# Closing quantised product of a fused transformer stack: the addition to X moved from GpSimd to VectorE, the exponents' scaling moved to ScalarE, exponent bits taken ahead

## What is computed

```
def quant_fp8(x):
    amax = jnp.max(jnp.abs(x)).astype(jnp.float32)
    scale = jnp.minimum(FP8_MAX / jnp.maximum(amax, 1e-12), FP8_MAX)
    x_fp8 = jnp.clip(x * scale, -FP8_MAX, FP8_MAX).astype(jnp.float8_e4m3fn)
    return (x_fp8, 1.0 / scale)
x2d = input.reshape(-1, weight.shape[1])          # layernorm(x), 4096 x 256
w_fp8, w_scale = quant_fp8(weight)                # 256 x 256
x_fp8, x_scale = quant_fp8(x2d)
acc = jnp.matmul(x_fp8.astype(jnp.float32), w_fp8.astype(jnp.float32).T)
out2d = (acc * (x_scale * w_scale) + bias).astype(jnp.bfloat16)
x = x + out2d
```

## Time and profile before

| what | value |
|---|---|
| median of 3 runs | 3275.01 us (3274.55 to 3279.48) |
| the profiled execution, own time | 3275.65 us |
| its span in the trace | 3273.9 us |
| PE busy | 2807.5 us (86%) |
| DVE busy | 1943.4 us (59%) |
| ACT busy | 1666.0 us (51%) |
| POOL busy | 1142.5 us (35%) |

### The profile page before, as it was taken

The page is one execution under the profiler, slowest core; times in us unless marked ns, Lnnn a source line. Parts: engine busy times, 40 slices in busy tenths (PEclk is TensorE's granted clock), DMA queues, the critical chain, the costliest instruction groups (busy, mean ns, idle before and its releaser), DMA issues. The chain is left out here.

```text
span 3273.9 us, 69748 instructions
## 1 busy us (share of the span) xinstructions
PE 2807.5 (86%) x26085; PEld 1890.0 (58%) x26085; DVE 1943.4 (59%) x4348; ACT 1666.0 (51%) x3073; POOL 1142.5 (35%) x1192
## 2 busy tenths in 40 slices
PE   4989695888789999999979989988569959999993
PEld 2554363555346666666645556666369946666672
DVE  4888565888555343443348887777554344555547
ACT  2778342777544444444427776766455513333332
POOL 6653008787000000000043334555410074565523
PEclk7999896999889999999979999999789978999995
DMA  3332002222214000000011211112243343332301
GB/s 116 76 74 61 14 1 96 67 67 64 45 52 155 1 1 1 1 1 1 1 57 57 73 54 42 47 56 67 87 140 92 91 115 69 80 84 63 78 21 51
DMA packets 164742, 189.86 MB, mean 58 GB/s; under 512 B 25969, under 2 KB 136833, under 8 KB 164257
## 3 DMA queue, kind: packets, MB, share of 16 engines
q1 hardware_dynamic: 147520, 143.44, 14.9%
q0 software_dynamic: 16896, 41.97, 4.9%
HBM read 67.09 MB, written 41.42 MB: 33 GB/s over the span
## 5 line engine op out<-in xcount | busy, mean ns | idle before, releaser
L1966 DVE TENSOR_TENSOR f1H<-f1HF,f1H 128x512 bf16<-128x512 f32 x256 | 176.6, 692 | 398.2 <-ACT f1H L1806 398.2
L1739 PE MATMUL ps<-f1xT,f1w 128*128 128x512 bf16 x1536 | 378.4, 383 | 6.2 <-ACT f1H L1806 6.2
L1761 PE MATMUL ps<-f1w,f1H 128*128 128x256 bf16 x3072 | 378.3, 273 | 0.0
L1761 PEld LDWEIGHTS ps<-f1w,f1H 128*128 128x128 bf16 x3072 | 301.4, 98 | 90.3 <-issue 1.1
L1803 ACT ACTIVATE f1HF<-ps 128x512 f32<-128x512 f32 x256 | 152.8, 597 | 333.9 <-PE ps L1739 333.8
L1103 ACT ACTIVATE a2PT<-ps 128x512 f32<-128x512 f32 (+1 forms) x512 | 259.7, 542 | 82.7 <-PE ps L917 59.5
L1739 PEld LDWEIGHTS ps<-f1xT,f1w 128*128 128x128 bf16 x1536 | 148.2, 98 | 151.0 <-issue 16.6
L756 POOL TENSOR_TENSOR a2RS<-a2VE,neghalf 128x4 f32<-128x4 f32 x32 | 32.7, 1022 | 530.5 <-DVE a2VE L1332 530.5
L894 PE MATMUL ps<-a2KS,a2QS 49*128 49x256 bf16 (+1 forms) x1024 | 173.6, 263 | 49.3 <-DVE a2NM L1256 19.7
L1649 POOL TENSOR_TENSOR f1RS<-f1VE,neghalf 128x4 f32<-128x4 f32 x8 | 8.1, 1011 | 572.6 <-DVE f1VE L1949 572.6
L1256 DVE TENSOR_REDUCE a1NM<-ps 128x2 f32<-128x512 f32 x256 | 166.0, 686 | 42.1 <-PE ps L894 41.0
(11 more groups left out here) (536 smaller groups left out, 7014.5 us busy)
## 6 DMA issues: line engine op xcount, KB each, us to landing
a2KS<-a2KH SPq DMA_DIRECT2D x192, 64.0 KB
a2QS<-a2QH SPq DMA_DIRECT2D x192, 64.0 KB
a4KS<-a4KH SPq DMA_DIRECT2D x96, 128.0 KB
a4QS<-a4QH POOLq DMA_DIRECT2D x96, 128.0 KB, 4.3
slots<-zeros SPq DMA_DIRECT2D x1, 9984.0 KB, 31.9
f2XG<-slots SPq DMA_DIRECT2D x39, 256.0 KB, 2.9
results<-f2OB SPq DMA_DIRECT2D x39, 256.0 KB, 2.1
f1WF<-in_f_w SPq DMA_DIRECT2D x32, 256.0 KB, 2.7
```

The costliest lines, as they stand in the source:

```text
L1739: m = nc.tensor.matmul(ps[:, (u * NCH + i) % 2, :], w1[:, x, kt, i * P:i * P + P], xT[:, half, y, kt, :], start=(j == 0), stop=(j == len(t ...
L1761: m = nc.tensor.matmul(out, H[:, (u * NCH + i) % HR, x, t * P:t * P + P], w2[:, y, i, :], start=first, stop=(f == YC - 1 and j == 2 and no ...
L1966: nc.vector.tensor_tensor(H[:, (u * NCH + i) % HR, 1, :], HF[:, (u * NCH + i) % 2, :], H[:, (u * NCH + i) % HR, 0, :], SUB).then_inc(S["h_ ...
```

## The change

On VectorE, the exponent bits of unit n+2 are taken (`bits`) into a T2 that now has two halves, right behind the rescaling of unit n-1; `quantise` is left with two instructions, clip and add, and a subtraction that is now a plain `tensor_tensor`. The scaling of the exponents is done by ScalarE in two instructions: `Relu(bits * S - L)` and then `+ L`, with L = 2^-6 x S, which is the same as max(bits, 2^-6) * S. The two constants are written by two small memsets ahead of VectorE's first reciprocal. GpSimd has no list in this block any more; VectorE adds OB to X (`added`) behind `bits`. ScalarE's order within a unit becomes exponents of unit n+1, scaling of unit n+2, then the PSUM copy of unit n. The weights are quantised before unit 0 instead of after it. SyncE's and TensorE's lists stay as they are.

```
-            @block.gpsimd
-            def _(pool):
-                for n in range(UNITS):
-                    pool.wait_ge(S["q_ob"].sem, S["q_ob"].at(n, 1))
-                    if n + 2 < UNITS:
-                        pool.wait_ge(S["q_step"].sem, S["q_step"].at(n + 2, 2))
-                    done = S["q_done%d" % (n % 2)]
-                    pool.wait_ge(done.sem, done.at(n // 2 - 1, 1))
-                    nc.gpsimd.tensor_tensor(OUT[:, n % 2]..., flat(X, n), OB[:, n % 2], ADD).then_inc(S["q_out"].sem, 1)
...
             @block.scalar
...
+                def exponents(n):
+                    t2 = T2[:, n % 2]
+                    act.wait_ge(S["q_bits"].sem, S["q_bits"].at(n, 1))
+                    nc.scalar.activation(t2, t2, ACT.Relu, scale=TO_FP8, bias=LEAST[:, 0:1]).then_inc(S["q_exp"].sem, 1)
+                    act.wait_ge(S["q_exp"].sem, S["q_exp"].at(n, 1))
+                    nc.scalar.activation(t2, t2, ACT.Identity, bias=LEAST[:, 1:2]).then_inc(S["q_exp"].sem, 1)
...
                 scaled(0)
                 scaled(1)
+                exponents(0)
                 for n in range(UNITS):
+                    if n + 1 < UNITS:
+                        exponents(n + 1)
+                    if n + 2 < UNITS:
+                        scaled(n + 2)
                     act.wait_ge(S["q_T"].sem, S["q_T"].at(n, 1))
                     act.wait_ge(S["q_acc"].sem, S["q_acc"].at(n - 2, 1))
                     nc.scalar.activation(QT[:, n % 2, :], ps[:, 6 + n % 2, :].bitcast(BF16), ACT.Copy
                                          ).then_inc(S["q_Tc"].sem, 1)
-                    if n + 2 < UNITS:
-                        scaled(n + 2)
...
+                def bits(n):
+                    dve.wait_ge(S["q_scaled"].sem, S["q_scaled"].at(n, 1))
+                    dve.wait_ge(S["q_ready"].sem, S["q_ready"].at(n - 2, 1))
+                    nc.vector.tensor_scalar(T2[:, n % 2].bitcast(I32), T1[:, n % 2].bitcast(I32), 0x7F800000, None,
+                                            ALU.bitwise_and).then_inc(S["q_bits"].sem, 1)
                 def quantise(n):
+                    step, t1, t2 = S["q_step"], T1[:, n % 2], T2[:, n % 2]
+                    dve.wait_ge(S["q_exp"].sem, S["q_exp"].at(n, 2))
+                    nc.vector.scalar_tensor_tensor(t1, t1, -FP8_MAX, t2, MAX, ADD).then_inc(step.sem, 1)
                     dve.wait_ge(step.sem, step.at(n, 1))
-                    nc.vector.tensor_scalar(t2, t2, FP8_LEAST, TO_FP8, MAX, MUL).then_inc(step.sem, 1)
...
-                    nc.vector.scalar_tensor_tensor(Q[:], t1, 1.0, t2, MUL, SUB).then_inc(S["q_ready"].sem, 1)
+                    nc.vector.tensor_tensor(Q[:], t1, t2, SUB).then_inc(S["q_ready"].sem, 1)
                 def out(c):
                     dve.wait_ge(S["q_acc"].sem, S["q_acc"].at(c, 1))
-                    dve.wait_ge(S["q_out"].sem, S["q_out"].at(c - 2, 1))
...
+                def added(c):
+                    done = S["q_done%d" % (c % 2)]
+                    dve.wait_ge(S["q_ob"].sem, S["q_ob"].at(c, 1))
+                    dve.wait_ge(done.sem, done.at(c // 2 - 1, 1))
+                    nc.vector.tensor_tensor(OUT[:, c % 2]..., flat(X, c), OB[:, c % 2], ADD).then_inc(S["q_out"].sem, 1)
...
+                nc.vector.memset(LEAST[:, 0:1], -FP8_LEAST * TO_FP8)
+                link(nc.vector.memset(LEAST[:, 1:2], FP8_LEAST * TO_FP8))
                 link(nc.vector.reciprocal(SC[:], ps[:, 4, P:P + 2]))
...
-                quantise(0)
-                weights()
+                bits(0)
+                bits(1)
+                weights()
+                quantise(0)
+                bits(2)
                 for n in range(1, UNITS):
                     quantise(n)
                     out(n - 1)
+                    if n + 2 < UNITS:
+                        bits(n + 2)
+                    added(n - 1)
                 out(UNITS - 1)
+                added(UNITS - 1)
```

More of the change, by code:

```diff
@@ L2283 @@
 FP8_LEAST = 2.0 ** -6
-Q8 = ["q_amax", "q_step", "q_scaled", "q_ready", "q_T", "q_Tc", "q_acc", "q_ob", "q_out", "w_step"]
+Q8 = ["q_amax", "q_bits", "q_exp", "q_step", "q_scaled", "q_ready", "q_T", "q_Tc", "q_acc", "q_ob", "q_out", "w_step"]
 Q8_DMA = ["q_in", "q_done0", "q_done1"]
@@ L2294, in quantised_linear @@
     for n in Q8 + Q8_DMA:
-        S[n].begin({"q_amax": 4, "q_step": 3, "w_step": 9}.get(n, 1))
+        S[n].begin({"q_amax": 4, "q_exp": 2, "w_step": 10}.get(n, 1))
     with ExitStack() as ctx:
@@ L2308, in quantised_linear @@
         T1 = sb("T1", [P, 2, UT * D], F32)
-        T2 = sb("T2", [P, UT * D], F32)
+        T2 = sb("T2", [P, 2, UT * D], F32)
+        LEAST = sb("LEAST", [P, 2], F32)
         Q = sb("Q", [P, UT * D], BF16)
@@ L2318, in quantised_linear @@
         with nc.Block() as block:
-            @block.gpsimd
-            def _(pool):
-                for n in range(UNITS):
-                    pool.wait_ge(S["q_ob"].sem, S["q_ob"].at(n, 1))
-                    if n + 2 < UNITS:
-                        pool.wait_ge(S["q_step"].sem, S["q_step"].at(n + 2, 2))
-                    done = S["q_done%d" % (n % 2)]
-                    pool.wait_ge(done.sem, done.at(n // 2 - 1, 1))
-                    nc.gpsimd.tensor_tensor(OUT[:, n % 2].rearrange("p t d -> p (t d)"), flat(X, n), OB[:, n % 2], ADD
-                                            ).then_inc(S["q_out"].sem, 1)
             @block.scalar
@@ L2335, in scaled @@
                                          ).then_inc(S["q_scaled"].sem, 1)
-                act.wait_ge(S["w_step"].sem, S["w_step"].at(0, 3))
+                def exponents(n):
[4 more added lines that the diff above has]
+                    nc.scalar.activation(t2, t2, ACT.Identity, bias=LEAST[:, 1:2]).then_inc(S["q_exp"].sem, 1)
+                act.wait_ge(S["w_step"].sem, S["w_step"].at(0, 4))
                 scaled(0)
                 scaled(1)
+                exponents(0)
                 for n in range(UNITS):
+                    if n + 1 < UNITS:
+                        exponents(n + 1)
+                    if n + 2 < UNITS:
+                        scaled(n + 2)
                     act.wait_ge(S["q_T"].sem, S["q_T"].at(n, 1))
@@ L2355, in link @@
                     dve.wait_ge(S["w_step"].sem, S["w_step"].at(0, links[0]))
-                def quantise(n):
[L2358 to L2362, removed]
+                def bits(n):
[3 more added lines that the diff above has]
+                                            ALU.bitwise_and).then_inc(S["q_bits"].sem, 1)
+                def quantise(n):
+                    step, t1, t2 = S["q_step"], T1[:, n % 2], T2[:, n % 2]
+                    dve.wait_ge(S["q_exp"].sem, S["q_exp"].at(n, 2))
+                    nc.vector.scalar_tensor_tensor(t1, t1, -FP8_MAX, t2, MAX, ADD).then_inc(step.sem, 1)
                     dve.wait_ge(step.sem, step.at(n, 1))
-                    nc.vector.tensor_scalar(t2, t2, FP8_LEAST, TO_FP8, MAX, MUL).then_inc(step.sem, 1)
-                    dve.wait_ge(step.sem, step.at(n, 2))
-                    nc.vector.scalar_tensor_tensor(t1, t1, -FP8_MAX, t2, MAX, ADD).then_inc(step.sem, 1)
-                    dve.wait_ge(step.sem, step.at(n, 3))
                     dve.wait_ge(S["q_T"].sem, S["q_T"].at(n - 1, 1))
-                    nc.vector.scalar_tensor_tensor(Q[:], t1, 1.0, t2, MUL, SUB).then_inc(S["q_ready"].sem, 1)
+                    nc.vector.tensor_tensor(Q[:], t1, t2, SUB).then_inc(S["q_ready"].sem, 1)
                 def weights():
@@ L2384, in out @@
                                                    MUL, ADD).then_inc(S["q_ob"].sem, 1)
+                def added(c):
+                    done = S["q_done%d" % (c % 2)]
+                    dve.wait_ge(S["q_ob"].sem, S["q_ob"].at(c, 1))
+                    dve.wait_ge(done.sem, done.at(c // 2 - 1, 1))
+                    nc.vector.tensor_tensor(OUT[:, c % 2].rearrange("p t d -> p (t d)"), flat(X, c), OB[:, c % 2], ADD
+                                            ).then_inc(S["q_out"].sem, 1)
                 nc.vector.tensor_reduce(q8["A2"][:, 0:1], q8["AM"][:], AX.X, MAX).then_inc(S["q_amax"].sem, 1)
@@ L2417, in linear @@
                     if c == 0:
-                        pe.wait_ge(S["w_step"].sem, S["w_step"].at(0, 9))
+                        pe.wait_ge(S["w_step"].sem, S["w_step"].at(0, 10))
                     pe.wait_ge(S["q_Tc"].sem, S["q_Tc"].at(c, 1))
```

## The result

The changed kernel takes 3263.11 us (median of 10 runs, 3257.99 to 3270.20); ten runs of the kernel before gave 3273.23 us (3267.36 to 3281.06). The ratio is 0.9966, 95% interval 0.9955 to 0.9977: 0.34% faster, between 0.23% and 0.45%. In us that is 11.1, between 7.5 and 14.7; the two medians differ by 10.1. The profiled execution took 3264.29 us, its span is 3262.5.

What follows compares the result with a forecast made beforehand. VectorE was taken as the bound, about 1.8 us of most units spent held by GpSimd's addition. Head +0.78, units -9.01 and tail -0.97 sum to -9.20; from 3275.01 that gives 3265.8 us, range 3262.5 to 3271.

Steps and rivals of the forecast that it cites:

- the last of the sum: Whole kernel: median 3275.01 less 9.20 gives 3265.8 us, with everything before 3208 us left alone.
- Prices: Block's instructions: subtraction and addition 1.23 us each on VectorE, ScalarE's two 1.14 each, two memsets 0.15.
- Head: Block's start to first rescaling: 0.78 us longer, the first rescaling coming at 3222.52 instead of 3221.74.
- The product's margin: Head of the block: TensorE's first product is ready 0.15 us before the first rescaling needs it.
- Units: First to seventh rescaling: five units of 5.44 us and one of 4.85, 32.05 against 41.06, so -9.01.
- Tail: After the seventh rescaling: VectorE's last addition starts 1.29 us after the last rescaling and takes 1.23; -0.97 us.
- The rule on ScalarE: Skill's advice of VectorE for relu, max, mul; claimed to cost nothing here while ScalarE's 1 us slack per unit holds.
- Dearer two-input instructions: Rival: VectorE's subtraction and addition take 1.70 us each, +7.1, giving 3272.9 us; chance 5%.
- The hold not GpSimd's: Rival: VectorE's subtraction stays at 3.02 us, +10.7, giving 3276.5 us, no difference; chance 2%.
- Tables: Rival: ScalarE loads tables three times per unit, 1.283 us each, and becomes the bound; 3284.5 us; chance 3%.
- The prediction's own sign: Part before the block: the forecast is wrong if the stretch before 3208 us moves by more than 3 us.
- Rival 4: Part before the block moves by some us or runs scatter, so the gain reads under 6.5 us; chance 10%.

Runs made afterwards that it cites:

- experiment 1: Kernel before without GpSimd's addition, output DMAs reading X: subtraction 1.22 to 1.23 us, first reduction to last rescaling's end 49.33 us against 60.15.
- experiment 2: Kernel before with only the addition moved from GpSimd to VectorE, behind the rescaling: block 58.19 us, 4.17 less than before.
- experiment 6: Changed kernel with one more ScalarE instruction per unit, a copy of the exponents onto themselves: block 54.69 us, 1.5 more.
- experiment 5: Changed kernel with ScalarE's PSUM copy put ahead of the scaling again: block 65.19 us, 12 more than the changed kernel's.
- experiment 8: Changed kernel again, on another chip: block 53.17 us, median 3266.37 us, ratio to the kernel before 0.9967.
- experiment 7: Changed kernel with half of units 0 to 5's additions on GpSimd beside the rescaling, unit 0 quantised earlier: block 48.91 us, median 3257.49, ratio to before 0.9946.
- experiment 4: Changed kernel with additions of units 0 to 5 on GpSimd, released when Q two units ahead is ready: block 50.85 us, 2.3 less.
- experiment 3: Changed kernel with the addition given back to GpSimd, released by the rescaling alone: block 58.61 us, 5.5 more than the changed kernel's.

## Where the prediction failed, and what held

The step that failed is the last of the sum, 3275.01 - 9.20 = 3265.8. It takes the median of three runs as the base, and it puts the 3208 us in front of the block at no change ("Everything before 3208 us is left alone"). The three runs lay 4.9 apart, and for the nothing no row was given. The changed kernel's median of 3263.11 is 2.70 us under the forecast. Of this 1.78 is the base, since ten runs put it at 3273.23, 0.02 is the block, and 0.90 lies in front of the block, where the sum had nothing. The ratio makes it more: 11.1 us under 3273.23 is 3262.1 (3258.5 to 3265.7), which is below the range's low end of 3262.5, and leaves 1.9 us for the part in front. The forecast of 3265.8 is just outside that interval.

The mechanism and the terms inside the block held, step by step:

- **Prices.** The plain subtraction is 1.225 and the addition 1.220 on average of eight each, taken as 1.23 from L2186. ScalarE's two are 1.14 and 1.15, taken as 1.14. The memsets add 0.12 (from the first reduction to the scale's multiplication, L2406, it is 1.85, before 1.73 with the earlier trace rows), taken as 0.15.
- **Head.** From the block's start to the first rescaling: 14.35, before 13.60. That is +0.75, forecast +0.78. ScalarE's scaling of unit 2 does wait for the first Q, and VectorE idles 1.22 for it. The product's margin, forecast 0.15, is 0.10: TensorE's first product ends at 3220.24 and the rescaling starts at 3220.34.
- **Units.** 3252.37 - 3220.34 = 32.03, forecast 32.05, before 41.06. The split is confirmed by experiments 1 and 2: the hold is GpSimd's.
- **Tail.** From the seventh rescaling to the end of the last addition 6.76, forecast 6.73.
- **The rule on ScalarE.** It speaks against Relu, max and mul on ScalarE. Experiment 6 shows that it doesn't hold here as long as the 1.1 us that ScalarE had left in a unit are not exceeded; no run went beyond them. Experiment 5 shows that ScalarE's load was not what needed care here, but its order. Leaving the exponents on VectorE was put at a gain of 3.4; experiment 2 does that and gained 4.17, because its head stays at 13.59.
- **Rivals.** Dearer two-input instructions: no, 1.22. The hold not GpSimd's: no, experiment 1. Tables: no load in the block. Of the two rows held against the tables one was no evidence: L2334 and L2343 are both Copy, so that the one follows the other without a load says nothing of Relu or Identity.

How much does the unchanged part in front move? In nine traces (all but experiment 1) the time of an execution is the block's start plus the block plus 5.13 to 5.17 us. Taking the block as the same in every run, a median time gives the block's start at the median: 3205.72 before and 3204.81 after in the ten runs each; on the other chip 3208.17 before, 3208.03 in experiment 8 and 3203.41 in experiment 7. So the front came out shorter in all three comparisons, by 0.9, 0.1 and 4.8. This is within the intervals: those of the first two ratios reach down to 7.5 and 6.2 us, and that of experiment 7 to 12.4, under the 13.5 of its block.

The traces show how the front drifts. This is one and the same instruction of VectorE, the 2107th of each trace, in the order before, after, experiment 8:

```profile
1268.83 0.69 DVE L1966 TENSOR_TENSOR f1H<-f1HF,f1H 128x512 bf16<-128x512 f32 x1 [1.91 <-ACT f1H L1806]
...
1263.12 0.69 DVE L1966 TENSOR_TENSOR f1H<-f1HF,f1H 128x512 bf16<-128x512 f32 x1 [1.91 <-ACT f1H L1806]
...
1266.16 0.69 DVE L1966 TENSOR_TENSOR f1H<-f1HF,f1H 128x512 bf16<-128x512 f32 x1 [1.91 <-ACT f1H L1806]
```

Against before it comes 5.71 earlier after the change and 2.67 earlier in experiment 8; at the block's start these have become 2.15 earlier and 0.73 later. So the same code drifts by several us and partly back within one execution. The two executions of the changed kernel (on two chips) are 3.04 apart at this instruction and 2.88 at the block's start, more than the 2.15 between before and after. In the six traces on chips of this speed the block starts at 3205.71, 3205.99, 3208.14 (before), 3208.70, 3208.87 and 3209.90. What causes this drift stays open, and so does whether the change moves the front by an us or two: no shift is shown, and none is excluded. My low bound allowed 3 us of drift from a base of three runs; single runs of one kernel span 12 us (3257.99 to 3270.20), so it was cut too close to the forecast for what the argument didn't cover. The prediction's own sign, a move of more than 3 us in the traces, did not show. Rival 4 priced such drift only as a gain that reads too small, not as one that reads too large.

## What to carry to other kernels

An engine can be the bound with 99% busy time (6.80 of 6.90 us here) and yet wait inside an instruction: look for one operation of one shape with two durations, and ask what another engine was doing at its end. To take GpSimd's work onto the engine that is the bound can pay, when the work holds that engine longer than it costs there; and GpSimd can still be of use if its piece is cut to the length of an instruction that doesn't collide. When work moves to an engine with slack, look at its place in that engine's order before its time: here a changed order cost 12 us (experiment 5), one more instruction 1.5 (experiment 6). And a forecast of a few us in 3270 stands on its base: take that from as many runs as the drift of the untouched part asks for, and give the range that drift on both sides.

## What the runs showed of the hardware

- A held VectorE instruction ended 1.08 us after GpSimd's end if it takes 1.23 alone, and 0.55 after if it takes 0.69 alone. That is 0.14 to 0.15 less than its own time, in both; what that part is, no row shows.
- The exponent bits, with one SBUF input, are held by GpSimd and hold it (1.59 for 0.69 in experiment 4, and 0.5 more on GpSimd in experiment 3). The rescaling, with its large input in PSUM and a small one in SBUF, keeps its 1.28 and leaves GpSimd its 2.12 and 1.16, in experiments 4 and 7. GpSimd starts second in all these rows; a rescaling that starts while GpSimd is at work was not seen.
- GpSimd's addition is 2.12 us for 1024 elements and 1.16 for 512; VectorE's is 1.22 and 0.68.
